# Attention: rotary swap by a matrix product with a signed permutation, and one mask product for two score tiles

## What is computed

```python
q = (x @ Wq).reshape(Bd, Sd, H, DH + D_ROPE)        # H 16, DH 16, D_ROPE 64
q_nope, q_rope = (q[..., :DH], q[..., DH:])
c_kv = x @ Wdkv                                      # 64 wide
kv = (c_kv @ Wukv).reshape(Bd, Sd, H, 2 * DH)
k_nope, v = (kv[..., :DH], kv[..., DH:])
k_rope = x @ Wkr                                     # one for all heads
def _rotate_half(x):
    x1, x2 = jnp.split(x, 2, axis=-1)
    return jnp.concatenate([-x2, x1], axis=-1)
def _apply_rope(x, cos, sin):
    return x * cos + _rotate_half(x) * sin
scores = einsum(q_nope, k_nope) + einsum(_apply_rope(q_rope), _apply_rope(k_rope))
attn = softmax(where(causal, scores * scale, -1e9))
out = einsum(attn, v).reshape(Bd, Sd, H * DH) @ Wo
```

## Time and profile before

| | |
|---|---|
| median of three runs | 1441.34 us |
| the profiled execution | 1443.96 us |
| its span, first to last instruction | 1442.2 us |
| mean granted clock of PE, share of full speed | 0.92 |
| busy over the span: PE, DVE, ACT, POOL | 1169.6 (81%), 985.1 (68%), 647.3 (45%), 599.3 (42%) us |
| `ln0` and its weight splits | about 14 to 34 us of the span |
| attention, jobs ahead of the loop | about 35 to 62 us |
| attention, the 64 steps | 62.8 to about 432 us |

### The profile page before, as it was taken

One profiled execution on the slowest core, in us unless ns is written; L12 is line 12 of the kernel. 1 busy time (PEld: TensorE's weight loads), 2 busy tenths in 40 slices (PEclk: granted clock), 3 DMA queues, 4 the chain that ended last, 5 costly groups with the idle time before them and its releaser, 6 DMA issues. The chain is left out here.

```text
span 1442.2 us, 32153 instructions
## 1 busy us (share of the span) xinstructions
PE 1169.6 (81%) x12288; PEld 881.9 (61%) x12288; DVE 985.1 (68%) x2082; ACT 647.3 (45%) x1519; POOL 599.3 (42%) x525
## 2 busy tenths in 40 slices
PE   2789898998874599998817885998999648999992
PEld 1356566665653398987713553665766527989882
DVE  6479798887786556456565956788797574555554
ACT  4367566666564133333446653353333223333342
POOL 0245445545430234334300195688696213333220
PEclk9899999999995599999958998999999759999996
DMA  4655756656533598876240002000000039966635
GB/s 158 155 131 157 175 167 172 167 164 158 147 111 87 197 419 345 277 248 252 66 173 8 15 25 45 16 17 2 2 2 2 27 93 397 419 238 243 253 99 186
DMA packets 98186, 216.83 MB, mean 150 GB/s; under 512 B 28977, under 2 KB 68146, under 8 KB 91890
## 3 DMA queue, kind: packets, MB, share of 16 engines
q1 hardware_dynamic: 88434, 192.22, 41.0%
q0 software_dynamic: 7488, 20.46, 4.2%
q10 hardware_dynamic: 2112, 2.10, 0.4%
HBM read 157.40 MB, written 40.04 MB: 137 GB/s over the span
## 5 line engine op out<-in xcount | busy, mean ns | idle before, releaser
L1228 ACT ACTIVATE ffn_h<-ffn_bank,ffn_b 128x256 f32<-128x256 f32 (+1 forms) x384 | 143.9, 431 | 278.5 <-PE ffn_bank L118 259.3
L1407 DVE CAST ffn_hh<-ffn_h 128x512 f16<-128x512 f32 (+1 forms) x192 | 80.7, 420 | 182.8 <-ACT ffn_h L1228 166.5
L116 PE MATMUL ffn_bank<-ffn_hh,ffn_W 128*128 128x256 f16 (+1 forms) x768 | 181.0, 254 | 8.9 <-DVE ffn_hl L1409 8.9
L1042 POOL DMA_INDIRECT ffn_xs<-xn_rows,ffn_from_rows x78 | 79.4, 1019 | 244.4 <-PE ffn_bank L1123 158.2
L118 PE MATMUL ffn_bank<-ffn_hh,ffn_W 128*128 128x256 f16 (+1 forms) x768 | 180.8, 254 | 0.0
L117 PE MATMUL ffn_bank<-ffn_hl,ffn_W 128*128 128x256 f16 (+1 forms) x768 | 180.7, 253 | 0.0
L644 ACT ACTIVATE att_prob<-att_bank,att_nmax 128x512 f32<-128x512 f32 (+3 forms) x256 | 127.1, 525 | 31.3 <-DVE att_nmax L726 30.0
L733 DVE TENSOR_TENSOR att_ptl<-att_bank,att_pth 128x384 f16<-128x384 f32 (+1 forms) x192 | 113.9, 593 | 34.4 <-ACT att_pth L651 34.4
L651 ACT ACTIVATE att_pth<-att_bank 128x384 f16<-128x384 f32 (+1 forms) x192 | 101.3, 528 | 79.0 <-PE att_bank L591 79.0
L1049 POOL DMA_INDIRECT y_rows<-ffn_y,ffn_to_rows x78 | 77.4, 993 | 133.6 <-DVE ffn_y L1418 86.9
L591 PE MATMUL att_bank<-main_identf,att_prob 128*128 128x128 f32 x640 | 99.6, 281 | 35.7 <-ACT att_prob L644 19.6
(11 more groups left out here) (345 smaller groups left out, 3222.6 us busy)
## 6 DMA issues: line engine op xcount, KB each, us to landing
ffn_W<-split_w SPq DMA_DIRECT2D x46, 2048.0 KB, 19.3
att_piece<-in_ffn_w SPq DMA_DIRECT2D x32, 512.0 KB, 5.2
split_w<-att_halves SPq DMA_DIRECT2D x32, 512.0 KB, 4.2
att_Q<-att_pair SPq DMA_DIRECT2D x64, 128.0 KB, 2.4
ffn_back<-y_rows SPq DMA_DIRECT2D x16, 512.0 KB, 9.1
att_KB<-att_krl SPq DMA_DIRECT2D x8, 512.0 KB, 5.6
att_Q<-att_pair SPq DMA_DIRECT2D x64, 64.0 KB, 2.1
xn_rows<-ffn_XN SPq DMA_DIRECT2D x8, 512.0 KB, 2.6
```

The costliest lines, as they stand in the source:

```text
L116: pe.matmul(out, ah, bh, start=start, stop=False)
L1228: ins_ = act.activation(h[layer][:, m, 0:n], bank[1 + 2 * layer + u][:, (m % 2) * n:(m % 2 + 1) * n], ACT.Gelu, bias=bias[:, ds(e + m, 1)])
```

## The change

It has four parts.

1. The weights `wt` and the swapped key columns of `wx` are gone. The second half of a rotary job is now two products in float32 (`turn_half`): the stationary matrix `swap` (a permutation by which rows change places within 64, with sign -1) with x times `sinT`, and the identity with x times `cosT`, both summed in bank 1.
2. DVE does both table products on bank 0, one behind the other, in the first drain of the job. PE's second half waits for them (`first_drained`), and for `swap`, made once.
3. POOL's `sum_rope` is gone. ACT copies bank 1 twice, to float16 and to the float32 tensor `rope`, in the place of the other jobs' second half; POOL's `low_rope` stays. In `START`, PE issues each job's first half ahead of the second half of the job before.
4. Score group 2 gets one mask product of 256 columns in place of two of 128.

```diff
+            def turn_half(job):
+                at = turn[job] % 2
+                pe.wait_ge(swap_made, 2)
+                pe.wait_ge(first_drained, nth[job] + 1)
+                pe.matmul(bank[1][:, :], swap[:, :], turned[:, at, 1, :], start=True, stop=False)
+                return pe.matmul(bank[1][:, :], identf[:, :], turned[:, at, 0, :], start=False, stop=True)
...
-                if what == "pair":
-                    ins = project(bank[1][:, :], wth, wtl, n % (NH // 2) * P, P, n // (NH // 2))
-                elif what == "kr":
-                    ins = project(bank[1][:, :], wxh, wxl, KT_AT, P, n)
+                if what in ("pair", "kr"):
+                    ins = turn_half(job)
...
-                    pe.matmul(out, Q[:, h, 0, q], KA[:, b % 2, 0:n], start=True, stop=False)
+                    pe.matmul(out, Q[:, h, 0, q], KA[:, b % 2, 0:n], start=at == 0, stop=False)
                     pe.matmul(out, Q[0:QK, h, 1, q], KB[0:QK, h, 0:n], start=False, stop=False)
-                    ins = pe.matmul(out[:, n - P:n], identb[:, :], upper_neg[:, :], start=False, stop=True)
-                ins.then_inc(score_ready, 1)
+                d = tiles[0][0] * P
+                pe.matmul(bank[bk][:, d:d + len(tiles) * P].rearrange("p (x n) -> p x n", n=P), identb[:, :],
+                          upper_neg[:, :].unsqueeze(1).broadcast_to([P, len(tiles), P]), start=False, stop=True).then_inc(score_ready, 1)
...
-            for job in START:
-                first_half(job)
+            first_half(START[0])
+            for job, following in zip(START, START[1:] + [None]):
+                first_half(following)
                 second_half(job)
...
             def high_rope(job):
-                act.wait_ge(summed, r + 1)
+                act.wait_ge(second_ready, nth_second[job] + 1)
                 if what == "kr":
-                    ins = act.activation(KA[:, n % 2, :], rope[:, r % 2, :], ACT.Copy)
+                    ins = act.activation(KA[:, n % 2, :], bank[1][:, :], ACT.Copy)
...
-                    ins = act.activation(pair[:, n % 2, 0, :], rope[:, r % 2, :], ACT.Copy)
+                    ins = act.activation(pair[:, n % 2, 0, :], bank[1][:, :], ACT.Copy)
                 ins.then_inc(rope_high, 1)
+                if r >= 2:
+                    act.wait_ge(rope_low, r - 1)
+                act.activation(rope[:, r % 2, :], bank[1][:, :], ACT.Copy).then_inc(second_drained, 1)
...
+                    for at, table in enumerate((cosT, sinT)):
+                        to = turned[:, r % 2, at, :]
+                        if what == "kr":
+                            ins = dve.scalar_tensor_tensor(to, bank[0][:, :], ATT_SCALE, table[:, :], ALU.mult, ALU.mult)
+                        else:
+                            ins = dve.tensor_tensor(to, bank[0][:, :], table[:, :], ALU.mult)
...
-                pool.tensor_tensor(rope[:, r % 2, :], turned[:, r % 2, 0, :], turned[:, r % 2, 1, :], ALU.add).then_inc(summed, 1)
```

More of the change, by code:

```diff
@@ L318, in attention_stage @@
         turned, rope = t.sb("turned", [P, 2, 2, S]), t.sb("rope", [P, 2, S])
-        pair = t.sb("pair", [P, 2, 2, S], F16)
+        pair, swap = t.sb("pair", [P, 2, 2, S], F16), t.sb("swap", [P, P])
         qnh, qnl, knh, knl = (t.sb(n, [P, 2, S], F16) for n in ("qnh", "qnl", "knh", "knl"))
@@ L367, in attention_stage @@
         nth_second = {job: n for n, job in enumerate(j for j in done if j[0] != "lat")}
-        turn = {job: n for n, job in enumerate(j for j in done if j[0] in ("pair", "kr"))}
+        ropes = [j for j in done if j[0] in ("pair", "kr")]
+        turn = {job: n for n, job in enumerate(ropes)}
         def wait_drained(eng, job):
@@ L655, in high_half @@
                 what, n = job
+                if what in ("pair", "kr"):
+                    if x:
+                        high_rope(job)
+                    return
                 if what not in ("lat", "qn", "kn", "v", "oT") or (what == "lat" and x):
@@ L678, in high_rope @@
                 what, n = job
-                if what not in ("pair", "kr"):
-                    return
                 r = turn[job]
-                act.wait_ge(summed, r + 1)
+                act.wait_ge(second_ready, nth_second[job] + 1)
                 if what == "kr":
-                    ins = act.activation(KA[:, n % 2, :], rope[:, r % 2, :], ACT.Copy)
+                    ins = act.activation(KA[:, n % 2, :], bank[1][:, :], ACT.Copy)
                 else:
@@ L693, in _ @@
                 high_half(job, 1)
-                high_rope(job)
             probs(0, 0)
@@ L708, in _ @@
                 high_probs(g, 2)
-                if last:
-                    high_rope(last)
                 if more:
@@ L717, in _ @@
         def _(dve):
+            halves_of = lambda a: a[:, :].rearrange("p (b x r) -> p b x r", x=2, r=HALF)
+            for x in range(2):
+                dve.tensor_scalar(halves_of(swap)[:, :, x, :], halves_of(identf)[:, :, 1 - x, :], -1.0, None, ALU.mult).then_inc(swap_made, 1)
             dve.memset(zeros[:, :], 0.0).then_inc(zeros_made, 1)
@@ L755, in drain @@
                 what, n = job
-                if what == "lat" and x:
+                if what in ("lat", "pair", "kr") and x:
                     return
@@ L763, in drain @@
                 if what in ("pair", "kr"):
-                    r, table = turn[job], sinT if x else cosT
+                    r = turn[job]
                     if r >= 2:
-                        dve.wait_ge(summed, r - 1)
-                    to = turned[:, r % 2, x, :]
-                    if what == "kr":
-                        ins = dve.scalar_tensor_tensor(to, bank[x][:, :], ATT_SCALE, table[:, :], ALU.mult, ALU.mult)
-                    else:
-                        ins = dve.tensor_tensor(to, bank[x][:, :], table[:, :], ALU.mult)
+                        dve.wait_ge(second_ready, nth_second[ropes[r - 2]] + 1)
+                    for at, table in enumerate((cosT, sinT)):
[4 more added lines that the diff above has]
+                            ins = dve.tensor_tensor(to, bank[0][:, :], table[:, :], ALU.mult)
                 elif what == "op":
@@ L826, in _ @@
         def _(pool):
-            def sum_rope(job):
-                what, n = job
-                if what not in ("pair", "kr"):
-                    return
-                r = turn[job]
-                wait_alone(pool, first_drained, nth[job] + 1, passed)
-                wait_alone(pool, second_drained, nth_second[job] + 1, passed)
-                if r >= 2:
-                    wait_alone(pool, rope_high, r - 1, passed)
-                pool.tensor_tensor(rope[:, r % 2, :], turned[:, r % 2, 0, :], turned[:, r % 2, 1, :], ALU.add).then_inc(summed, 1)
             def low_rope(job):
@@ L843, in low_rope @@
                 wait_alone(pool, rope_high, r + 1, passed)
+                wait_alone(pool, second_drained, nth_second[job] + 1, passed)
                 if what == "kr":
@@ L864, in _ @@
             for job in START:
-                sum_rope(job)
                 low_rope(job)
@@ L869, in _ @@
                 if last:
-                    sum_rope(last)
                     low_rope(last)
@@ L2408, in attention_layer @@
         parts = [
[L2409 removed]
+            (rows(ins["att_rope"]), *wr), (rows(ins["att_mixed"]), *wx),
             (ins["att_up"], *wu), (rows(ins["L0_attn_a_Wo"]), *wo)]
         layer_norm_stage(nc, "ln0", X, XTh, XTl, c["identf"], lambda t: SplitWeights(t, parts))
[L2412 removed]
+        attention_stage(nc, X, XTh, XTl, (wr, wx, wu, wo), c["identf"], identb, upper_neg, cosT, sinT, ffn_w,
                         split_w, nope, xn_rows)
@@ L2451, in attention_weights @@
     rope, nope = q[:, :, DH:], q[:, :, :DH].reshape(D, NH * DH)
-    swap = lambda w: np.concatenate([w[..., HALF:], w[..., :HALF]], axis=-1)
-    turned = np.stack([rope.reshape(D, NH * DR), swap(rope).reshape(D, NH * DR)])
-    mixed = np.concatenate([nope, Wdkv, Wkr, Wkr, swap(Wkr), swap(Wkr)], axis=1)
+    mixed = np.concatenate([nope, Wdkv, Wkr, Wkr], axis=1)
     up = Wukv.reshape(LAT, NH, 2, DH).transpose(0, 2, 1, 3).reshape(LAT, 2 * NH * DH)
-    return {"att_turned": turned, "att_mixed": mixed, "att_up": up}
+    return {"att_rope": rope.reshape(D, NH * DR), "att_mixed": mixed, "att_up": up}
 def ssm_weights(W_in, conv_w, conv_b, D, norm_w, W_out, mup_vector):
```

10 lines of the change are left out of this document (4 added, 6 removed).

## The result

The changed kernel takes 1526.2 us (median of four, 1524.57 to 1527.09), the kernel before 1442.08 us in runs beside it: ratio 1.058, interval 1.055 to 1.061. That is 84 us slower, where 40 were forecast and 1503 us was the upper end. The direction was right, the size was half.

What follows compares the result with a forecast made beforehand. PE and DVE were taken as near full, even steps bound by PE, odd ones by POOL's late sum. Terms 36 + 3.6 - 3 + 0 + 5 - 2 = +39.6 us gave 1481 us; forecast 1465 to 1496, 8-in-10 range 1460 to 1503.

Steps and rivals of the forecast that it cites:

- The float32 product: Rotary jobs' second half on PE: 0.43 us a product, so 1.30 us falls to 0.86, 0.44 less per job.
- the rule of the Trainium skill: Rival for the float32 products: four passes, 0.86 us each, 31 us more in all, 1512 us; chance 0.02.
- The wait: PE stands 1.6 us for DVE's table products in even steps: +1.2 us each, +36 us for 30 pair jobs.
- That it can't shrink in steady state: Table products follow group 1's maximum, which waits for PE, so the even step costs +0.9 to +1.2 us.
- half of it is absorbed: Rival: the loop adapts, a pair of steps costs 0.2 us, 1450 us in all; chance 0.09.
- Odd steps: Loop's odd steps: 0 with six-product halves, +0.1 us with shorter jobs, -0.55 without a job; -3 us in sum.
- The kr steps: Three kr jobs in odd steps of the loop, delayed like the pair jobs: +3.6 us in all.
- the rival of the clock: Rival: half of 30 even steps start a stretch at 1.2 GHz, 21 us more, 1502 us; chance 0.12.
- Ahead of the loop: Start before the first scores: the new job order delays the rotary key, +5 us, ends +2 and +7.
- `ln0`: Layer norm stage: ACT loses the copy of `wt` and 256 of 1152 columns, -2 us, ends -1 and -3.
- the walk: Start followed instruction by instruction with earlier durations: subtraction done at 58.3 in place of 52.92, +5.4 us.
- The mask product: Score group 2 in 64 steps: columns remain, one instruction goes, between 0 and -3.5 us; taken as 0.

Runs made afterwards that it cites:

- e1: Changed kernel with the rotation's two products in float16 (table products, permutation and identity in float16), same waits: ratio 1.0248, median 1478.99 us.
- e6: Changed kernel with both table products moved early on DVE, ahead of the sums and the maximum of group 1: ratio 1.0266, median 1480.67 us.
- e5: Changed kernel with the order ahead of the loop put back, each job's second half right behind its first: ratio 1.0504, median 1516.04 us.
- e12b: Changed kernel, float32 products kept, with table products early on DVE and the old order ahead of the loop: ratio 1.0226, median 1469.92 us.
- e11b: Kernel before the change with ACT's copy of the rotary sum one step later, behind the exponential of group 2: ratio 1.0137, median 1457.55 us.
- e9: Changed kernel with float16 products, table products early on DVE and the old order ahead of the loop: ratio 0.9993, median 1444.0 us.

## Why the prediction was wrong, point by point

**The float32 product, the step that failed.** The prediction took "four float32 products in 1.88 us" from the earlier trace rows and got 0.43 us for one. The arithmetic was right, the count was not: the row counts instructions that the chip ran, and a float32 product is two of them. It takes 0.86 us, so the second half grew by 0.42 us where I had it shrink by 0.44. I then used the same row to set aside the rule of the Trainium skill ("FP8 and Floating Point Precision", section "TensorE Precision Notes": true FP32 makes four passes through the array) and gave it 0.02. By that rule a product would take 4 x 0.215 = 0.86 us, an estimate, and the trace agrees: 0.94 and 0.85 us for the two (131.87 to 132.81 to 133.66). Of the 44 us by which the forecast was short this term is 28 by its own working (33 x 0.86). The whole price of float32 against float16 is 47 of the 84 us by experiment e1, which takes PE's second half from 1.72 to 0.43.

**The wait** was forecast with its place, cause and length: 1.6 us of standing, idle time "some 50 us in all"; measured 48.8 us in 33 waits, and 52 us when taken away. The table products started 3.55 us behind the step's first DVE instruction (126.90), not 3.32 as in the earlier trace rows, and the signal and PE's restart took 0.14 us, not 0.05: 0.3 us a step, 10 us in all. With the products (0.93 us in this step) this is the difference between the 6.78 (5.58 + 1.2) forecast for step 8 and the 8.03 that it took.

**That it can't shrink in steady state** was right for the order as written. But it rested on DVE's order, and e6 shows how little holds it there. The rival "half of it is absorbed" did not occur.

**Odd steps.** Forecast: 0 with long halves, +0.1 with short ones, -0.55 without a job. Measured 0 with long halves (qn 5.52 and 5.52); +0.40 for lat, kn and oT (5.48 against 5.08) but -0.7 for v (5.49 against 6.21); and without a job -0.20 where the kernel before takes 5.08, more where it takes 5.24 to 6.88 (steps 3, 15, 31, 47). The wait of DVE for ACT was right (0.69 us, 136.91, against my 3.30 behind the turns' start: 3.25). The odd steps that are not kr's changed by -4.5 us in sum, close to the -3 forecast, but this is luck: no single kind but the long one came out as forecast, and there are nine steps without a job, not eight.

**The kr steps.** Forecast +1.2 us each. Measured 7.99 us for two of them and 9.69 for the third (5.52 before), and the even steps behind them took 9.6 to 10.3 us against 8.07, since each of the three ran into a stretch at 1.2 GHz. These are three places with two thin steps in a row.

**The loop by kinds of step.** Of the +70.1 us, 27 even steps that don't stand behind kr have +50.2 (forecast 32.4), the three kr steps and the three behind them +22.5 (forecast 7.2), the other odd ones -4.5 (forecast -3) and the end of the loop +1.8. Most of the 27 grew by 2.0 to 2.5 us, but six (2, 14, 16, 48, 54, 56) by only 0.5 to 0.7: they took 7.4 to 7.6 us in the kernel before, with the granted clock lowered, and ran at full clock in after.

**The clock.** I took no change in sum. Such a case in after, around the products at 161.97 (columns as in rows 10):

```profile
160.00:163.10 3.10, 1.13 (x3) 0.68 (x4) 2.81 (x6) 0.54 (x1) 2.67 (x2) 1.00 0.66 125
163.10:166.50 3.40, 3.40 (x11) 1.95 (x10) 0.42 (x1) 1.05 (x3) 0.00 (x0) 0.51 1.10 186
```

PE is busy 1.13 of 3.10 us and the next stretch runs at 1.2 GHz, as in the earlier trace rows. The mean granted clock over the span is 0.92 in both kernels, and over the loop 0.97 before and 0.98 after. So the rival of the clock did not occur in sum: the stretches at 1.2 GHz moved, mostly from the six even steps named above to the kr places. That the float32 products, which keep PE busy, are the reason is likely and not shown.

**Ahead of the loop.** Forecast +5 and -2; measured, from e5, +9.8 and -2.1. The chain was right up to the latent: its products start at 37.32 (39.3 less the 2 us of `ln0`). Behind it, with gaps of 2.09 and 1.42 us on PE ahead of kn's and kr's first halves, PE ran at 1.2 GHz through both:

```profile
43.00:51.00 8.00, 5.55 (x12) 1.29 (x12) 1.23 (x2) 0.91 (x2) 0.00 (x0) 0.57 0.20 66
```

The next pair's first half starts at 53.26, where the walk, less the 2 us, has 51.6. Its six products take 1.9 us and not 1.3, in part at 1.2 GHz, and kr's float32 products behind them take 2.78 us where the walk has 1.0:

```profile
55.19 1.91 PE L514 MATMUL att_bank<-att_turned,att_swap 128*128 128x512 f32 x2
...
56.89 1.24 PE L515 MATMUL att_bank<-att_turned,main_identf 128*128 128x512 f32 x2
...
57.97 0.38 PE L116 MATMUL att_bank<-attw_XTh,attw_wrh 128*128 128x512 f16 x1
```

Two copies and the subtraction last until 60.68, 2.7 us and not 2.4. These four make 4.4 of the 4.8 us missed; the walk itself gave 5.4 where I took 5.

**The mask product** (0) and **`ln0`** (-2) were right.

**What is left.** 2.6 us fall behind the loop, where nothing was changed. Between kernels that share this code the stretch behind the loop took from 1007 us (e12b) to 1018 us (e5), against 1013.9 before and 1016.5 in after, and I don't explain it.

## What to carry to other kernels

Before a price is read off a row, the row's count has to be held against what the program issues there: here a count that was double said that one instruction of the program is two on the chip. When a product of one engine's result is placed back on the engine that feeds it, count the places between: here the table products sat behind a maximum that waits for PE, and three places forward were worth 45 us, nearly as much as float16 in place of float32 products (47). When an instruction is moved in time, look also at what its followers on other engines will then run beside: a copy moved by less than a step on ACT cost 20 us, since it brought POOL's long subtraction next to DVE's multiplication. And an engine with 16% of idle time can take no more in one step if the idle time lies in another: with both table products in the even step, DVE bound it at 5.8 us even with PE's work and wait gone.

## What the runs showed of the hardware

A multiplication on DVE of 64 elements a partition takes 0.21 us alone and 0.58 to 0.78 us when POOL's float32 to float16 copy of 1024 elements runs beside it, in all 30 cases of after (in the kernel before, beside POOL's addition, mostly 0.32). One such case in the timeline of after:

```profile
137.78 1.03 POOL L862 CAST att_halves<-att_piece 128x1024 f16<-128x1024 f32 x1
...
138.31 0.59 DVE L764 TENSOR_TENSOR att_O<-att_both,att_rinv 128x64 f32<-128x64 f32 x1
...
138.82 0.68 DVE L798 SCALAR_TENSOR_TENSOR att_knl<-att_bank,att_knh 128x512 f16<-128x512 f32 x1
```

The copy ends at 138.81 and DVE's next instruction starts at 138.82, so the multiplication ends as the copy does. The Trainium skill ("SBUF — State Buffer", section "Who interferes with whom") says that a DVE instruction with two SBUF inputs and a GpSimd instruction that reads SBUF need the same port pair and that the later one waits for the whole of the earlier one. The trace agrees: both operands, `both` and `rinv`, lie in SBUF. The rows of e11b show the same with POOL's subtraction of 1024 elements, which reads SBUF too: 2.13 us on POOL, 2.19 us on DVE for the multiplication that starts 0.02 us later. In e9 and e12b the same meeting in steps 12, 28 and 44 makes it 1.9 us.

With `sum_rope` gone, POOL comes to the copy just when DVE normalises, in every odd step up to 59 but the three with kr. It is the likely rest of the +0.40 us in the steps with lat, kn and oT; in those with qn and op it changes nothing (5.52 and 5.55 as before). No run moved this copy alone, so its share is argued from the trace and not shown.
